# Deformable sampling on Trainium2: one accumulator bank for the turned samples in place of two, copied one tap behind the weighings

## What is computed

```python
def bilinear_sample(x, py, px):
    ...
    return v00 * (1 - wy) * (1 - wx) + v01 * (1 - wy) * wx + v10 * wy * (1 - wx) + v11 * wy * wx

def deform_conv(x, off_w, off_b, mod_w, mod_b, reg_w, k, pad):
    offset = conv2d(x, off_w, off_b, pad)
    mask = 2.0 * jax.nn.sigmoid(conv2d(x, mod_w, mod_b, pad))
    ...
    sampled = bilinear_sample(x, py, px) * mask[:, None]
    return jnp.einsum('bckhw,ock->bohw', sampled, reg_w.reshape(O, C, k * k))
```

## Time and profile before

| | |
|---|---|
| median of 3 runs | 7189.62 us |
| lowest and highest | 7186.41, 7193.9 us |
| the profiled execution | 7190.81 us |
| its span in the trace | 7189.0 us |
| granted TensorE clock, mean of the span | 0.917 |
| busy: PE, DVE, ACT, POOL | 72%, 75%, 62%, 67% |
| HBM traffic | 194 GB/s over the span |

### The profile page before, as it was taken

The page is one execution under the profiler, slowest core; times in us unless marked ns, Lnnn a source line. Parts: engine busy times, 40 slices in busy tenths (PEclk is TensorE's granted clock), DMA queues, the critical chain, the costliest instruction groups (busy, mean ns, idle before and its releaser), DMA issues. The chain is left out here.

```text
span 7189.0 us, 96561 instructions
## 1 busy us (share of the span) xinstructions
PE 5186.9 (72%) x22687; PEld 3143.4 (44%) x22687; DVE 5423.3 (75%) x10561; ACT 4492.4 (62%) x11845; POOL 4824.1 (67%) x4571
## 2 busy tenths in 40 slices
PE   7777676776766666666676766676889966757768
PEld 6444444444444344443444443332544434645644
DVE  5777777777777777777777777773769988988972
ACT  4666666666666666666666666775337758958940
POOL 3777777777777777777777777772029965945920
PEclk9999999999999999999999999887999987987989
DMA  7887887878878788787887878886000011231234
GB/s 220 285 250 239 248 250 236 251 238 248 250 237 250 239 248 251 236 251 239 248 251 236 251 238 246 293 284 203 28 21 33 33 49 49 103 110 60 103 122 165
DMA packets 584384, 1400.46 MB, mean 195 GB/s; under 512 B 94035, under 2 KB 258144, under 8 KB 579424
## 3 DMA queue, kind: packets, MB, share of 16 engines
q0 software_dynamic: 308224, 1006.95, 46.3%
q1 hardware_dynamic: 273506, 385.08, 15.8%
q10 hardware_dynamic: 2304, 4.20, 0.2%
HBM read 1314.13 MB, written 81.67 MB: 194 GB/s over the span
## 5 line engine op out<-in xcount | busy, mean ns | idle before, releaser
L627 POOL DMA_INDIRECT st_corners<-corner_table,df_rows x3840 | 3637.9, 947 | 1266.4 <-issue 1048.9
L1000 ACT ACTIVATE st_corners<-st_corners,df_share 128x128 f32<-128x128 f32 x3840 | 1225.7, 390 | 1555.4 <-DMA st_corners<-corner_table,df_rows 1516.0
L900 PE MATMUL df_acc_ps<-df_turned,df_tapw 128*128 128x512 f32 x3840 | 2006.9, 649 | 38.8 <-DMA df_tapw<-in_tap_w_dram 35.4
L889 PE MATMUL df_turn_ps<-main_ident,df_sampled 128*128 128x128 f32 x3840 | 646.6, 295 | 1426.7 <-DVE df_sampled L673 1369.7
L889 PEld LDWEIGHTS df_turn_ps<-main_ident,df_sampled 128*128 128x128 f32 x3840 | 445.5, 148 | 2208.3 <-issue 2096.0
L668 DVE TENSOR_TENSOR st_corners<-st_corners,df_part_ps 128x512 f32<-128x512 f32 x960 | 660.3, 688 | 850.6 <-ACT df_part_ps L1000 838.2
L1000 ACT ACTIVATE df_part_ps<-st_corners,df_share 128x128 f32<-128x128 f32 x3840 | 1178.8, 351 | 35.2 <-DVE df_sampled L673 34.6
L173 PE MATMUL st_conv_ps<-st_ow,st_patch 128*128 128x147 f32 (+1 forms) x6272 | 994.0, 306 | 1.1 <-issue 1.1
L900 PEld LDWEIGHTS df_acc_ps<-df_turned,df_tapw 128*128 128x128 f32 x3840 | 737.5, 210 | 579.5 <-issue 538.7
L173 PEld LDWEIGHTS st_conv_ps<-st_ow,st_patch 128*128 128x128 f32 x6272 | 895.8, 201 | 9.6 <-issue 9.0
L657 DVE TENSOR_TENSOR st_corners<-st_corners,df_weight_ps 128x512 f32<-128x512 f32 x960 | 657.3, 685 | 275.0 <-DMA st_corners<-corner_table,df_rows 270.1
(11 more groups left out here) (373 smaller groups left out, 5613.9 us busy)
## 6 DMA issues: line engine op xcount, KB each, us to landing
df_tapw<-in_tap_w_dram SPq DMA_DIRECT2D x962, 128.0 KB
sc_c_row<-c SPq DMA_DIRECT2D x128, 512.0 KB, 3.6
st_corners<-corner_table,df_rows POOLq DMA_INDIRECT x3840
y_b<-st_outs SPq DMA_DIRECT2D x128, 256.0 KB, 5.2
l1f_w<-in_w_dram SPq DMA_DIRECT2D x32, 1024.0 KB, 6.9
fu_spare<-y_b SPq DMA_DIRECT2D x64, 256.0 KB, 5.4
f_y_in<-y_b SPq DMA_DIRECT2D x64, 256.0 KB, 5.7
u<-dw_u SPq DMA_DIRECT2D x64, 256.0 KB, 2.1
```

Of the source, the lines that this page charges most:

```text
L627: nc.gpsimd.indirect_dma_start(corners[slot][:, j].rearrange("p v c -> p (v c)"), None, tables[g // GPB], bass.IndirectOffsetOnAxis(ap=row ...
L889: t = nc.tensor.transpose(turn_ps[pair][:, j * TILE:(j + 1) * TILE], sampled[pair][:, j, :], ident[:])
L900: m = nc.tensor.matmul(acc_ps[:, h, :], tapw[pair][:, h * P:(h + 1) * P], turned_sb[pair][:], start=first, stop=last, skip_group_check=not ...
L1000: nc.scalar.activation(dst, src, ACT.Copy, scale=share[slot][:, j - VT, v:v + 1]).then_inc(weighed_a, 1)
```

## The change

`turn_ps` becomes one bank where it was two, with one memset less ahead of the stage. ScalarE's unit n copies tap n - 1 where it copied tap n - 2: a new constant BEHIND = 1 stands for this distance, LAG stays 2 elsewhere. `finish` copies the last tap of the old group in step 0 and the first tap of the new group in step 1. The semaphore `operand` now counts from 1 where it counted from 2, since one copy less runs ahead of tap 0. With this, the unchanged wait of `turn(n)` (`operand`, n + 1) means that tap n - 1 has been copied, where it meant tap n - 2; and the wait of `multiply(n)` becomes n + 2 and still means that tap n has been copied. The two conditions of `operands` keep their meaning. `turned_sb` keeps two buffers. TensorE's order stays: turn n, convolution, multiply n - 2.

```diff
--- before.py
+++ after.py
@@ -425,11 +425,12 @@
         f, k = divmod(at - FUSE_AT - shift, FUSE_EVERY)
         return (f, k) if 0 <= f < GPB else (None, None)
 
-    CLEARS = 3 + 3
+    CLEARS = 3 + 2
     LAST_TAP = [t0 + taps - 1 for t0, taps in zip(FIRST_TAP, TAPS_OF)]
     VT = TPG // 2
     AT = TPG - VT
     LAG = 2
+    BEHIND = 1
     ROWS = SPAN // W
     with ExitStack() as ctx:
         sb, pb, sem = tools(nc, ctx, "df")
@@ -466,7 +467,7 @@
         stats_f = sb("stats_f", [P, GPB * 6])
         mvf = sb("mvf", [P, 2])
         gmf = sb("gmf", [P, 2])
-        turn_ps = [pb(f"turn_ps{s}", [P, SPAN]) for s in range(2)]
+        turn_ps = pb("turn_ps", [P, SPAN])
         acc_ps = pb("acc_ps", [P, HALVES, SPAN])
         part_ps = pb("part_ps", [P, TPG, 2, P])
         weight_ps = pb("weight_ps", [P, 512])
@@ -850,8 +851,7 @@
             nc.vector.memset(first_sb[:, 0:GPB], float(QSIDE + 1)).then_inc(cleared, 1)
             nc.vector.memset(first_sb[:, GPB:], float(QSIDE + 1)).then_inc(cleared, 1)
             nc.vector.memset(acc_ps[:], 0.0).then_inc(cleared, 1)
-            for s in range(2):
-                nc.vector.memset(turn_ps[s][:], 0.0).then_inc(cleared, 1)
+            nc.vector.memset(turn_ps[:], 0.0).then_inc(cleared, 1)
             dve.wait_ge(cleared, CLEARS)
             dve.wait_ge(t.loaded, 16 * OFFSET_LOADS)
             positions(0)
@@ -886,14 +886,14 @@
                 pe.wait_ge(operand, n + 1)
                 pe.wait_ge(summed, n + SLOTS + 1)
                 for j in range(TPG):
-                    t = nc.tensor.transpose(turn_ps[pair][:, j * TILE:(j + 1) * TILE], sampled[pair][:, j, :],
+                    t = nc.tensor.transpose(turn_ps[:, j * TILE:(j + 1) * TILE], sampled[pair][:, j, :],
                                             ident[:])
                 t.then_inc(turned, 1)
 
             def multiply(g, tap, pair, use, first=False, last=False, br=0):
                 n = g * TAPS + tap
                 pe.wait_ge(tap_loaded[pair], (use + 1) * 16)
-                pe.wait_ge(operand, n + 3)
+                pe.wait_ge(operand, n + 2)
                 if first:
                     pe.wait_ge(acc_free, g * len(BRANCHES) + br + 3)
                 for h in range(HALVES):
@@ -1005,7 +1005,7 @@
 
                 act.wait_ge(multiplied, n + 3)
                 act.wait_ge(turned, n + 3)
-                nc.scalar.activation(turned_sb[pair][:], turn_ps[pair][:], ACT.Copy).then_inc(operand, 1)
+                nc.scalar.activation(turned_sb[pair][:], turn_ps[:], ACT.Copy).then_inc(operand, 1)
 
             def copy_out(g, br):
                 done = g * len(BRANCHES) + br
@@ -1028,7 +1028,10 @@
             def finish(g, step):
 
                 copy_out(g, len(BRANCHES) - 3 + step)
-                operands(g, TAPS - LAG + step, step)
+                if step < BEHIND:
+                    operands(g, TAPS - BEHIND + step, (TAPS - BEHIND + step) % 2)
+                elif g + 1 < GROUPS:
+                    operands(g + 1, step - BEHIND, (step - BEHIND) % 2)
                 if step == LAG - 1:
                     copy_out(g, len(BRANCHES) - 1)
 
@@ -1039,7 +1042,7 @@
                     return
                 if isinstance(tap, int) and tap - LAG - 1 in LAST_TAP:
                     copy_out(g, LAST_TAP.index(tap - LAG - 1))
-                operands(g, tap - LAG, pair)
+                operands(g, tap - BEHIND, 1 - pair)
 
             def hidden(at):
```

## The result

The changed kernel took 7221.8 us (median of 6 runs, 7215.69 to 7231.3), the kernel before 7190.49 us on the same chip (6 runs, 7184.93 to 7196.19): a ratio of 1.0044, 95% interval 1.0031 to 1.0057, or about 31 us more. Forecast were 7194.0 us and a range of 7182 to 7215. The profiled execution took 7224.41 us, its span is 7222.6 us against 7189.0.

A forecast was written before the change was run, and what follows sets the result against it. POOL's gathers, 5.0 us a tap and 4800 us in all, were taken as the bound. Group starts +1.3, +1.9 and +2.8, ends -1.1 and -0.5, sum to +4.4 us: 7194.0 us, range 7182 to 7215.

The forecast's parts named there:

- the least distance: From the end of tap n - 4's sum to POOL's first gather of tap n: at least 0.81 us.
- The ring: In settled taps, turn, convolution, multiply and copy form a closed ring of 4.2 us, covered by POOL's 5.0 a tap.
- the other fourteen group starts: Starts of all groups but 3 and 15: 0.2 us lost at each, 2.8 us together.
- the bound of 18 us: Upper bound for the fourteen group starts together, at group 3's 1.3 us for each.
- The loop: Catching up at group starts: turn to multiply, copy, weighings, additions and hand-overs take 9.0 us for two taps, 4.5 each.
- the ring becomes the bound while the clock is low: Rival: at 1.2 GHz a tap takes 5.8 us, eating 0.8 of slack; 40 us over group starts, 7230 us; chance 0.18.
- Group 3: At its start tap 4 is summed later, at 1050.0, so POOL begins tap 8 late: 1.3 us lost.
- Group 15: At its start a late weight delays the copy of tap 4, hence POOL's tap 10: 1.9 us lost.
- The end of the stage: Last two copies now stand ahead of the first and second copy_out: 1.1 us gained.
- The memset at the start: Ahead of the stage one of two memsets goes, which ScalarE and VectorE waited for: 0.5 us gained.
- The clock falls more often: Rival: twice the taps at TensorE's lower level, up to 90 us less what slack takes, 7250 us; chance 0.03.
- each turn waits a copy out: Rival: TensorE's idle time before turns does not cover the copy; 640 us more over 960 taps, 7830 us; chance 0.01.

The follow-up runs named there:

- e2: Changed kernel with four SBUF buffers for the turned samples instead of two, still one accumulator bank: 7190.82 us, ratio 1.0004 to the kernel before.
- e3: Changed kernel with TensorE's order convolution, multiply n - 2, turn n; one bank, two buffers: 7184.37 us, ratio 0.9997 to the kernel before.
- e11: Changed kernel without the two L1067 activations per unit of the fusing stage, semaphore only raised (result wrong): 7211.72 us, ratio 1.0033 to the kernel before.
- e4: Changed kernel without ScalarE's row shifts in units 54 to 57 of groups 0 to 13 (result wrong): 7201.46 us, ratio 1.0015 to the kernel before.
- e10: The changed kernel run again without any edit: 7218.76 us, ratio 1.0043 to the kernel before.
- e9: Changed kernel with idle TensorE transposes ahead of the turns of taps 52 to 55 and of turn 2: 7210.31 us, ratio 1.0029 to the kernel before.
- e1: Changed kernel with two accumulator banks again, ScalarE's new order kept: 7211.55 us, ratio 1.0047 to the kernel before.
- e7: Changed kernel with 40 idle transposes ahead of turn 2 of each group but the first: 7219.28 us, ratio 1.004 to the kernel before.
- e8: Changed kernel with multiply n - 2 ahead of turn n on TensorE and two accumulator banks: 7191.86 us, ratio 1.0 to the kernel before.
- e12: Changed kernel without the shifts of units 54 to 57 and without the L1067 activations (result wrong): 7196.9 us, ratio 1.0016 to the kernel before.
- e5: Changed kernel with each turn's four transposes done twice: 7214.6 us, ratio 1.0038 to the kernel before.
- e6: Kernel before the change with each turn's four transposes done twice: 7193.48 us, ratio 1.0001 to the kernel before.

## Why the prediction was wrong, and where it was right

**What bounds it, and what a settled tap costs: right.** POOL's gathers are the bound, the least distance is 0.81 us (in after 2250.39 to 2251.20, and in no trace is it less), settled taps cost nothing, and the copy's new wait of 1.2 us has the expected place. The ring of turn, convolution, multiply and copy was put at 4.2 us; the rows of after give 2429.64 to 2433.81, 4.17 us.

**The mechanism of the loss: right.** "Queued behind the waiting copy are the eight weighings, behind them VectorE's three additions, and behind those POOL's slot." e2 and e3 take away the copy's wait for the multiply, each in another way, and the loss with it. That SyncE's loads were charged nothing was right too: the multiplies' idle time for their weights fell, from 35.4 to 6.2 us.

**The step that failed** is the term "for the other fourteen group starts I take 0.2 us each, 2.8 us together", and under it the sentences "two taps take [...] 9.0 us, or 4.5 a tap. That is under 5.0, so the lateness dies out by 0.5 us a tap". Those fourteen starts (all but groups 3 and 15) cost 29.0 us more than before in one profile of the changed kernel and 17.4 in the other, ten and six times the 2.8; the bound of 18 us was too low for one of them. The loop's own length was about right: the lateness dies out from tap 6 to tap 14 as a loop of 8.7 us would have it. It was applied where it doesn't hold, and three things were left out:
- *Work behind the copy.* The loop counted turn to multiply, copy, weighings, additions. In units 54 to 57 the shifts (1.37 us), in the last groups the activations of L1067 (1.41 us) stand between the copy and the weighings. With 1.4 us more the loop is 10.4 us, 5.2 a tap, and that is above POOL's 5.0. e11 shows it for group 15; e4 shows that the shifts count at the groups' ends, together with the clock.
- *The clock.* The rival "the ring becomes the bound while the clock is low" had about the right price for a tap at 1.2 GHz, and looked at the start of the group alone. At the groups' ends it is the larger term. The prediction had 3.5 us from turn to multiply, and at tap 55 it is 6.58 (5.79 in e10). An estimate from these rows: two taps take 9.0 + 3.1 + 1.4 = 13.5 us, 3.5 more than POOL's 10.0, and from tap 55 to tap 57 the lateness did grow by 3.2 us (12.9 to 16.1). The same sum gives 2.7 for e10 (measured 2.7), 2.0 for e4, which has no shifts (1.95), and 1.3 for e9, which has a short turn to multiply (1.7); for e1, with two banks, it is further off, 1.4 (2.1). At tap 2 it gives +1.2 for after (measured +1.0 from tap 2 to tap 4) and -1.2 for e7 (-1.5).
- *Carry-over.* I looked at each start by itself, and at one sum in it (tap 4, in group 15 tap 6). The lateness that is made behind tap 55 reaches the next group, where tap 2 is late enough to hold up tap 6. In the mean of groups 1 to 13 the sum of tap 57 is 2.4 us later than before (16.1 against 13.7), that of tap 1 3.1 us (15.2 against 12.1), that of tap 4 5.3 us (20.6 against 15.3). The limit is 19.2 us of lateness, four taps of 5.0 less 0.81.

**The single terms.** Group 3: +1.3 forecast, all of it at tap 8; 0.8 measured in after, of which 0.5 at tap 6, and nothing in e10. It was not the tightest start either: ten of the groups 1 to 14 lost 1.7 to 3.7 us in after. Group 15: +1.9 forecast; 6.7 and 6.9 measured, of which e11 gives 5 to 6 us to the two activations of L1067, the bare loop that the forecast used leaves 0.8 to 1.7. Group 0, one of the fourteen, loses 0.8 us more than before in the one profile and 3.5 in the other. The end of the stage, -1.1: from the first gather of the last tap to the end of the last `copy_out` it is 22.4 us in after and 25.6 in e10, 27.0 before, so 1.4 to 4.6 us gained. In after a last multiply starts 0.15 us behind its `copy_out`, and the next `copy_out` 0.03 us behind that multiply, with no copy between, as forecast:

```profile
4959.20 1.02 ACT L1021 ACTIVATE st_outs<-df_acc_ps 128x1024 f32<-128x1024 f32 x1 [2.89 <-PE df_acc_ps L900]
4960.12 0.59 ACT L1008 ACTIVATE df_turned<-df_turn_ps 128x512 f32<-128x512 f32 x1
4960.37 1.96 PE L900 MATMUL df_acc_ps<-df_turned,df_tapw 128*128 128x512 f32 x4 [1.20 <-ACT st_outs L1021]
4962.36 1.02 ACT L1021 ACTIVATE st_outs<-df_acc_ps 128x1024 f32<-128x1024 f32 x1 [1.65 <-PE df_acc_ps L900]
```

The memset at the start, -0.5: the first gather is at 99.19 us in after, at 100.99 in e10 and at 100.99 before; it can't be told from nothing.

**The rivals.** The first (7230 us, chance 0.18) was nearest in place and size, 40 us against 31; of its cause, the clock, the runs bear out a part (e9), and the nearness of the number is in part luck: the rival had no shifts, no work of the fusing stage and no carry-over in it. *The clock falls more often* is not seen: the granted clock over the span is 0.916 and was 0.917. That each turn waits a copy out is refuted: the turn's idle time grew by 31.2 us in all (1426.7 to 1457.9), not by 640. The Trainium skill, page "PSUM — Partial Sum Buffer", summary of rules for kernel authors, advises another bank for an accumulator that is read while a matmul runs. The 640 us were the prediction's own reading of that rule. In this kernel a turn waits until the bank has been copied out, and that wait cost no time that the ratios show (e1 beside the changed kernel, e8 beside e3): TensorE is idle 1.04 and 1.15 us before a settled turn anyway, and a copy takes 0.60.

**What stays open.** How the 31 us divide between the clock, the shifts and `copy_out` (1.02 us each, in units 0 and 1) no run separates: e4 moved the clock too, e9 the waits for weights, and `copy_out` was never taken out. Of the 12 us that are left in e12 the same is true. Nor was it tried why the amount in the profile differs by 15 us between two executions of one kernel.

## What to carry to other kernels

When a wait is put ahead of other work in an in-order queue, cost the loop with everything that can stand between the wait and the work that the bound needs, in each kind of iteration, not in the plain one alone; a loop of 4.5 us a tap under a bound of 5.0 was turned into 5.2 by 1.4 us of unrelated activations, and into 6.8 where TensorE ran at its lower level too. Follow lateness across the boundary between groups, since it is paid where the slack runs out and not where it arises. And the single accumulator wasn't what made this kernel slow: one bank was free as soon as the copy no longer waited for a multiply, which a swap of two calls on TensorE gave.

## What the runs showed of the hardware

- More work on TensorE shortened the stretch that mattered most: with 0.46 us of work added, turn 55 to the end of its multiply took 4.28 us (e5) where it took 6.58 and 5.79. In the kernel before it did not: 5.82 us with the added work (e6), 5.57 without. The doubled turns raised the granted clock from 0.93 to 0.96 in the kernel as changed and from 0.94 to 0.96 in the one before, and the kernel with them was no slower.
- A turn behind a longer idle stretch of TensorE ran at the lower level: 3.54 us and 5.62 us idle, then 1.09 us each for four transposes, where 1.0 us idle is followed by 0.63. It isn't the idle time alone: in the kernel before turn 55 of group 1 took 1.09 us behind 0.8 us of idle. In e7 and e9, with transposes in that gap, turn 2 to the end of its multiply took 3.35 us in place of 5.73.
- The copy out of the accumulator takes 594 ns on average behind a wait for a multiply and 577 ns where it has none (e2, e3).
